# Edge groups: scale and beta written in place in PSUM, residual read from PSUM

## What is computed

```python
# layer 1: pooled messages, max per target node, then a residual block
e = x[src] * (1 + softplus(c) * edge_weight[:, None])
pooled = relu(layer_norm(e @ pool_w + pool_b) * g_p + b_p)
aggregate = segment_max(pooled, dst)            # 0 where a node has no edge
h = concat([x, aggregate]) @ final_w + final_b
x1 = layernorm(x + relu(layer_norm(h) * gamma + beta))
# layer 2: typed messages, mean per target node, root weight, residual
agg_b = segment_mean(comp[type, b] * x1[src], dst)       # b = 0..7
out = layernorm(x1 + concat(agg_b, x1) @ weight + bias)
```

## Time and profile before

| | |
|---|---|
| median of 3 runs | 912.48 us (911.65 to 912.67) |
| the profiled execution's own time | 910.83 us |
| its span in the trace | 909.0 us |
| busy share DVE, PE, POOL, ACT | 86%, 85%, 79%, 67% |
| mean granted clock of PE | 0.958 |

### The profile page before, as it was taken

The page is one execution under the profiler, slowest core; times in us unless marked ns, Lnnn a source line. Parts: engine busy times, 40 slices in busy tenths (PEclk is TensorE's granted clock), DMA queues, the critical chain, the costliest instruction groups (busy, mean ns, idle before and its releaser), DMA issues. The chain is left out here.

```text
span 909.0 us, 18559 instructions
## 1 busy us (share of the span) xinstructions
PE 769.2 (85%) x4588; PEld 566.3 (62%) x4588; DVE 777.6 (86%) x2823; ACT 610.0 (67%) x2862; POOL 717.8 (79%) x702
## 2 busy tenths in 40 slices
PE   5699999999999999999999988777299998988920
PEld 3577777777777777777778777666144444444410
DVE  6889999999999999999999979887179999989940
ACT  3799999999999999999999867776201111111120
POOL 2588888988989898898898667777777777777774
PEclk9999999999999999999999989999799999999975
DMA  4377676666666666666666422334188888877610
GB/s 114 111 230 236 193 234 209 197 213 206 207 199 215 205 201 207 208 205 198 203 205 200 123 67 86 101 107 177 46 293 272 304 295 286 300 276 286 230 47 27
DMA packets 88576, 175.46 MB, mean 193 GB/s; under 512 B 16716, under 2 KB 34024, under 8 KB 82199
## 3 DMA queue, kind: packets, MB, share of 16 engines
q1 hardware_dynamic: 71286, 144.02, 46.7%
q0 software_dynamic: 15744, 29.71, 10.8%
q10 hardware_dynamic: 1440, 0.56, 0.2%
HBM read 105.88 MB, written 70.88 MB: 194 GB/s over the span
## 5 line engine op out<-in xcount | busy, mean ns | idle before, releaser
L704 ACT ACTIVATE junk<-ps 128x128 bf16<-128x128 f32 x884 | 235.1, 301 | 30.1 <-PE ps L554 19.3
L704 ACT ACTIVATION_READ_ACCUMULATOR junk<-ps 128x1 f32 x884 | 206.7, 235 | 0.0
L656 PE MATMUL ps<-agg_all,w_cen 128*128 128x512 f32 (+1 forms) x400 | 176.0, 593 | 5.9 <-DVE agg_all L1185 5.1
L406 POOL DMA_INDIRECT x_dst<-in_x,dst_i x98 | 153.9, 1571 | 17.6 <-issue 7.7
L551 PE MATMUL ps<-w_cen,xT 128*128 128x128 f32 x984 | 160.2, 295 | 0.0
L436 POOL TENSOR_TENSOR work<-work,vec_raw 128x512 f32<-128x512 f32 x98 | 127.8, 1304 | 30.4 <-DVE work L1084 29.7
L551 PEld LDWEIGHTS ps<-w_cen,xT 128*128 128x128 f32 x984 | 129.9, 197 | 28.9 <-issue 28.9
L1185 DVE TENSOR_TENSOR agg_all<-coefs,ps 128x1024 f32<-128x1024 f32 x98 | 117.7, 1210 | 31.6 <-PE ps L642 18.3
L1084 DVE SCALAR_TENSOR_TENSOR work<-ps,st,vec_raw 128x128 f32<-128x128 f32 x492 | 137.8, 343 | 0.4 <-ACT st L719 0.3
L1016 DVE BATCH_NORM_STATS2 bn<-work 128x6 f32<-128x128 f32 x492 | 135.2, 280 | 1.2 <-DVE st L1004 0.6
L406 POOL DMA_INDIRECT x_table<-agg_all,scat_i x98 | 104.9, 1070 | 37.7 <-issue 28.3
(11 more groups left out here) (139 smaller groups left out, 1371.9 us busy)
## 6 DMA issues: line engine op xcount, KB each, us to landing
coefs<-coef_line SPq DMA_DIRECT2D x49, 1024.0 KB, 6.0
rows<-in_x SPq DMA_DIRECT2D x97, 256.0 KB
x_table<-work SPq DMA_DIRECT2D x97, 256.0 KB
out_rows<-outb SPq DMA_DIRECT2D x97, 256.0 KB
x_dst_table<-x_dst SPq DMA_DIRECT2D x98, 64.0 KB
rows<-x_dst_table SPq DMA_DIRECT2D x24, 256.0 KB
same_prev<-mask_line SPq DMA_DIRECT2D x7, 224.0 KB, 4.1
x_dst<-in_x,dst_i POOLq DMA_INDIRECT x98, 4.0
```

The lines of the kernel that those rows point to most:

```text
L406: return pool.indirect_dma_start(*args, bounds_check=last_node, oob_is_err=False)
L656: last = pe.matmul(MT[b][:, 0:n * D], w_cen[:, W_BASE + m, :], prod[:, b, m, 0:n, :].rearrange("p t d -> p (t d)"), start=(m == 0), stop=( ...
L704: last = nc.scalar.activation(junk[:, kind * CH + m, :], bank[:, cols(m, m + 1)], ACT.Square, accum_out=power[:, b, 1, TOP + kind * CH + m ...
```

## The change

For edge groups alone, `scaled` writes its product back into the PSUM bank that it reads, `edge_beta_added` adds beta there in place, and the residual reads its first input from that bank; its output still goes to the SBUF tile. PE's first product from edge group 2 on waits also for `dve_v`, the end of the residual of two groups before. No instruction is added, removed or moved on any engine; dense groups are as they were.

```diff
@@ PE, first product
                     need(pe, S["dve_t"], s - 2)
+                    if is_group(c, 3) and not is_dense(c, 3):
+                        pe.wait_ge(S["dve_v"], s - 2)
@@ DVE, residual()
-                        dve.scalar_tensor_tensor(h, h, 0.0,
+                        dve.scalar_tensor_tensor(h, h if is_dense(c, 3) else H[1 - b], 0.0,
                                                  rows[:, (c - 3) % SLOTS, 0:CH, :].rearrange("p c d -> p (c d)"),
                                                  ALU.max, ALU.add).then_inc(S["dve_v"], 1)
@@ DVE, scaled()
                         for m in range(CH):
-                            last = dve.scalar_tensor_tensor(hn[:, (c - 2) % SLOTS, m, :], H[b][:, cols(m, m + 1)],
+                            h = H[b][:, cols(m, m + 1)]
+                            last = dve.scalar_tensor_tensor(hn[:, (c - 2) % SLOTS, m, :] if is_dense(c, 2) else h, h,
                                                             st[:, 7, TOP + m:TOP + m + 1], vec_raw[:, GAM_F, :],
                                                             ALU.mult, ALU.mult)
@@ DVE, edge_beta_added()
-                        h = hn[:, (c - 2) % SLOTS, :, :]
+                        h = H[b].rearrange("p (c d) -> p c d", c=CH)
                         dve.wait_ge(S["dve_t"], s - 1)
                         own.mark(dve.tensor_tensor(
                             h, h, vec_raw[:, BET_F:BET_F + 1, :].broadcast_to([P, CH, D]), ALU.add))
```

## The result

The changed kernel takes **906.61 us** (median of 5 runs, 905.47 to 907.05) against 912.67 us (911.65 to 914.93, 5 runs) for the kernel before: a ratio of 0.9924, with a 95% interval of 0.9907 to 0.9942. (The ratios are as recorded and not quotients of the medians, which here give 0.9934.) It is faster by 6.1 us in the medians.

The account below looks back on a forecast made before the run. POOL's edge-group scatters, held 8.6 us by DVE instructions with two SBUF inputs, set the end. Gains of 2.0 + 0.8 + 2.7 = 5.5, plus 0.5 - 0.1, give 5.9 us: 912.48 - 5.9 = 906.6 us, whole range 904.0 to 911.2.

Parts of the forecast that it names:

- The holds: Edge groups' scatters on POOL: DVE instructions with two SBUF inputs hold them, 8.6 us together; PSUM operands end most.
- Rival 4: POOL's scatters: something other than the second SBUF input holds them, so no gain, 912.5 us; chance 7%.
- My count of starts: Of 98 edge-group scatters, 21 start inside L1116, L1103 or L1030, six of them in L1116; all 17 over 1.1 us included.
- DVE's price: DVE's edge-group instructions with PSUM operands: taken as 0 extra each, between -10 and 90 ns.
- Rival 3: DVE in edge groups: PSUM operands cost more, deciding from 85 ns an instruction; 912.8 to 915.5 us at 90 ns; chance 12%.
- Start: Edge groups 0 to 2, through first product 7 to group 5: 2.0 us of removed scatter delay arrive whole.
- clock: PE at half clock, 529.3 to 536.0 us: a shorter idle gap ahead gains 0.8 us, between 0 and 2.1.
- The added wait: PE's first products waiting for the residual of two groups before: costed at nothing, 2.1 us if uncovered.
- cover: ACT reaches the delayed squares only after making x1, and DVE needs them a step later; hides 2.1 us of waiting.
- Rival 2: PE's first products: their new wait for residuals puts 2.1 us on the path; gain 3.8, 908.7 us; chance 8%.
- Middle: 537.5 to 603.1 us, DVE sets the pace: 6.0 us mostly become slack; waits of 1.08 and 1.66 go, gaining 2.7 us.
- end: From group 20: x1's feed stays last, 5.5 us earlier; the last window gains 0.5 us more, less 0.1 for L1116.

Follow-up runs that it names:

- Experiment 2: Kernel before with edge groups' scale in place in PSUM, beta add reading PSUM but writing SBUF, old residual, PE waiting for the beta add: 909.13 us, ratio 0.9947.
- Experiment 3: Changed kernel with the scale going to SBUF, beta add from there into PSUM, residual reading PSUM, PE's added wait kept: 910.81 us, ratio 0.9968.
- Experiment 4: Changed kernel with DVE's side work of steps 108 to 117 moved behind the next step's residual: 903.11 us, ratio 0.9892.

## Why the prediction was right, and where it was not

**The holds (right).** Of 8.6 us 7.9 are gone. Experiments 2 and 3 each leave 5 us less of holds than before and gain 0.53% and 0.32%; the changed kernel leaves 7.9 less and gains 0.76%. Their scatter phases are shorter by 5.0, 3.9 and 5.2 us. With the wait alone nothing is gained. The long scatters left in experiments 2 and 3 start inside the instructions that kept two SBUF inputs, and in no other, which shows what holds POOL. The instructions with PSUM operands are no faster (350, 691, 682 ns), so the gain doesn't come from them as such. Experiment 2 is the plainest: only operands differ, and a wait that ended none of PE's idle time, and with 5 us less of holds the scatter phase is 5.0 us shorter. What the engines' steps gain or lose by merely falling differently was not tested; the holds alone moved by 2.4 us that way. Rival 4 falls.

My count of starts was a little low: 24 scatters start inside the three kinds of instruction, not 21, and seven in L1116, not six. The three more start in the instruction's last 0.06 us or first 0.01 us and take 0.98 us, and all 17 long ones are among the 24 as said.

**DVE's price (right).** 33 ns for each edge group, 0.4 us over the 11.5 groups where DVE sets the pace. Rival 3 needed 85 ns an instruction; it was 5 to 6 on average. By the table in the Trainium skill, "VectorE: DVE Perf Modes", section "The TRN2 errata", I had estimated 65 ns more for a PSUM input. The trace disagrees: the residual takes 682 ns with an input from PSUM and 684 ns with both from SBUF in dense groups.

**Start and clock (the sum nearly right, the start over-sized, the clock's part under-sized).** Group 5's first scatter in the timeline, and the window in which PE ran at half clock before (columns as in the earlier trace rows):

```profile
536.09 0.99 POOL L406 DMA_INDIRECT x_table<-agg_all,scat_i  x1 [0.37 <-issue]
```

```profile
529.30:536.00 6.70, 6.70 (x54) 5.72 (x52) 6.19 (x26) 5.89 (x23) 4.92 (x5) 1.00 0.24 75
```

The clock is 1.00 there, against 0.51. First product 7 now starts at 528.00 without a wait for a landing, and PE had no idle gap ahead of it. Counted from the first scatter, first product 7 starts 1.1 us earlier (19.7 us after it, against 20.8), where I had 2.0, and group 5 starts 3.4 us earlier (27.8 against 31.2), where I had 2.0 + 0.8. So the stretch between the two, where the clock changed, gave about 2.4 us, not 0.8 and slightly more than my upper bound of 2.1.

**The added wait (the step that failed).** I costed it at nothing, with 2.1 us should its cover be gone. PE's and DVE's timelines of the changed kernel:

```profile
548.81 0.37 PE L551 MATMUL ps<-bias,ones 3*128 3x512 bf16 x1 [1.27 <-DVE work L1032]
...
555.66 0.37 PE L551 MATMUL ps<-bias,ones 3*128 3x512 bf16 x1 [2.24 <-DVE work L1032]
...
561.52 0.37 PE L551 MATMUL ps<-bias,ones 3*128 3x512 bf16 x1 [1.65 <-DVE work L1032]
```

```profile
552.88 0.16 DVE L928 COPY carry_col<-ps 98x1 f32<-98x1 f32 x1 [1.16 <-PE ps L613]
554.73 0.68 DVE L1032 SCALAR_TENSOR_TENSOR work<-ps,rows 128x512 f32<-128x512 f32 x1
```

The three first products are the ones that I named, but PE waits 5.2 us for them, since it now arrives earlier. And the cover had a hole: I looked at the squares, which DVE needs a step later. DVE's side work waits for a small matmul of PE in the *same* step (L613, the carries), and that stands in PE's queue behind the first product that waits for the residual. So DVE waited for PE, and its next residual, for which PE waits again, came later. POOL then waited 2.06 us for x1 of group 9 and 0.93 us for group 10. Rival 2 was thus partly true at the same time as the forecast. Its price: 1.1 us between the scatter phases of experiments 2 and 3 with equal holds. Experiment 4 gets back 3.5 us in the medians; how much of that is the wait and how much the place of the side work could not be split on the first chip (on the second the move alone brings nothing, 1.0022 and 1.0028).

**Middle and end (over-sized).** Counted from the first scatter, first product 20 starts 5.5 us earlier (90.1 us after it, against 95.5), as I had for the whole loop. But group 20's first scatter starts only 4.4 us earlier (111.1 against 115.5). POOL waited 3.29 us for it, so the feed was last there, as said. The 1.0 us lost between the two is a step that the prediction didn't have. PE waits for the rows' transfer just ahead of first product 22 in both kernels, and runs at about half clock behind it. The changed kernel, then the kernel before (timeline, and windows as in the earlier trace rows):

```profile
609.22 1.09 PE L537 MATMUL ps<-ident,rows 128*128 128x128 f32 x4 [2.66 <-DMA rows<-x_dst_table]
610.23:614.60 4.37, 4.37 (x20) 3.93 (x20) 1.19 (x6) 0.60 (x2) 3.46 (x4) 0.50 1.03 411
```

```profile
613.50 0.63 PE L537 MATMUL ps<-ident,rows 128*128 128x128 f32 x4 [2.50 <-DMA rows<-x_dst_table]
614.06:617.90 3.84, 3.84 (x20) 3.61 (x20) 1.32 (x6) 0.59 (x2) 2.92 (x4) 0.59 1.03 405
```

The 20 matmuls from there on take 4.37 us at a clock of 0.50 and 3.84 us at 0.59. That is half of the 1.0 us; the rest stays open. With the end's 0.8 us (I had 0.5 - 0.1) the whole phase is 5.2 us shorter instead of 5.9.

So the time of 906.6 rests on one term that was too small (the clock) and on others that were too large (start and middle) or missing (the wait, the slower clock near the end), which nearly cancelled. The trace's 5.2 us and the medians' 6.1 us lie on either side of the 5.9, so the closeness is luck in part. And it holds for the first chip.

## What to carry to other kernels

Where GpSimd issues indirect transfers back to back, look at which VectorE instruction its long ones start in. Here a VectorE instruction with two SBUF inputs at that moment held it until about the end of the last one in a row, by up to 0.76 us, and moving one input to PSUM ended that at 33 ns for six instructions. Working in place in PSUM keeps a bank longer, though: look at everything that stands in the matmul queue behind the new wait, small matmuls for side work included, and put the release of the bank ahead of side work. This advice rests on one chip: the changed kernel with that order was 1.1% slower on the other (with `LEAD = 6`), for a reason that stays open. Compare on more than one chip before adopting such a change.

## What was not expected of the hardware

- Whether a scatter is held depends on its start: the scatter at 538.08, with a residual starting 0.04 us after it, takes 0.98 us; the one at 550.23, 0.07 us into a residual, takes 1.50 us. The edge isn't sharp: 0.03 us into such an instruction one scatter takes 1.51 us (632.90, before) and another 0.98 us (517.70, changed kernel). And a short instruction with two SBUF inputs (0.34 us) became a hold of 0.70 us because the next such instruction followed it without a gap (before):

```profile
596.87 0.34 DVE L1116 SCALAR_TENSOR_TENSOR agg_all<-work,st 128x128 f32<-128x128 f32 x1
596.99 1.68 POOL L406 DMA_INDIRECT x_table<-agg_all,scat_i  x1 [0.30 <-issue]
597.13 0.68 DVE L1103 TENSOR_TENSOR work<-work,vec_raw 128x512 f32<-128x512 f32 x1
```

- The second chip took 991 us for the kernel before. The dense groups took nearly as long as on the first (the changed kernel's first scatter starts at 514.4 against 508.3 us); the rest comes after them. In the edge groups ACT stopped for up to 7.6 us with no releaser on the core in the changed kernel, and from the last scatter to the end of the span it took 306 us (700.8 to 1006.4) against 264 us on the first chip. There POOL's gathers waited 22.9 us in the same way, so it isn't ACT alone. The change's sign differed between the chips.
